# Graph-network megakernel on Trainium2: adjacency products of the first stage moved ahead, bias terms in two buffers on three engines

## What is computed

```python
def L0(x, adj_in, adj_out, bias_in, bias_out, gate_w_in, gate_b_in, gate_w_out, gate_b_out, loop_gate):
    msg_in  = (einsum('nm,bmd->bnd', adj_in, x)  + bias_in)  * sigmoid(x @ gate_w_in  + gate_b_in)
    msg_out = (einsum('nm,bmd->bnd', adj_out, x) + bias_out) * sigmoid(x @ gate_w_out + gate_b_out)
    msg_loop = x * sigmoid(x @ loop_gate)
    return relu(msg_in + msg_out + msg_loop)
def L1(features, A, W1, ...):
    A_norm = A + eye(n)
    deg = A_norm.sum(0) + A_norm.sum(1) - diagonal(A_norm)
    A_hat = A_norm * rsqrt(deg)[:, None] * rsqrt(deg)[None, :]
    agg = einsum('nm,bmd->bnd', A_hat, features)
    h = relu(batchnorm(agg @ W1.T + b1)); ...
x = layernorm(x + L0(x, adj, adj, ...))
x = layernorm(x + L1(x, adj, ...))
x = layernorm(x + L2(x, adj, ...))
x = layernorm(x + L3(x, adj, ...))
```

## Time and profile before

| | us |
|---|---|
| median of three runs | 679.86 |
| lowest and highest | 679.27, 680.56 |
| the profiled execution | 680.88 |
| its span, first to last instruction | 678.9 |
| mean granted TensorE clock | 0.989 |

### The profile page before, as it was taken

How to read it: one execution, slowest core, us unless ns; L and a number is a source line. 1 busy time by engine, 2 the same in 40 slices (tenths; PEclk the granted TensorE clock), 3 DMA queues, 4 the chain that set the end, 5 groups by cost and what they waited for, 6 DMA issues and landing times.

```text
span 678.9 us, 9236 instructions
## 1 busy us (share of the span) xinstructions
PE 632.6 (93%) x2698; PEld 435.5 (64%) x2698; DVE 475.9 (70%) x1510; ACT 426.8 (63%) x921; POOL 243.6 (36%) x262
## 2 busy tenths in 40 slices
PE   7899988997799999999999999999999999999993
PEld 5655746445585587578657757765775686576572
DVE  5977885778886657876876787688668765463354
ACT  3667766764846676675667577666857666446552
POOL 4599982004644031324506232440523243021031
PEclk7999999999999999999999999999999999999997
DMA  8224000000000000000000000000000000000000
GB/s 339 94 96 180 4 1 0 1 0 1 0 1 1 0 1 1 1 1 31 2 0 1 31 1 1 31 1 0 2 31 1 1 31 1 0 2 31 1 31 31
DMA packets 4225, 16.80 MB, mean 25 GB/s; under 512 B 464, under 2 KB 464, under 8 KB 4048
## 3 DMA queue, kind: packets, MB, share of 16 engines
q1 hardware_dynamic: 4176, 16.23, 6.2%
HBM read 12.03 MB, written 4.19 MB: 24 GB/s over the span
## 4 chain that ended last, share of the span: by engine, by line
PE 60%; DVE 13%; ACT 7%; issue 3%; POOL 1%; DVEq 0%; ACTq 0%; POOLq 0%
PE QQ L783 23%; PE QQ L795 14%; PE QQ L634 4%; PE PA L738 4%; PE PA L766 4%; PE PB L757 2%; DVE raw L1472 2%; ACT raw L1044 2%; DVE HT L1450 2%; ACT raw L1051 2%; DVE raw L1468 2%; ACT HB L1012 2%; PE PB L719 1%; PE PB L805 1%; PE PA L719 1%
## 5 line engine op out<-in xcount | busy, mean ns | idle before, releaser
L1044 ACT ACTIVATE raw<-QQ,BL 128x256 f32<-128x256 f32 (+2 forms) x312 | 168.8, 562 | 95.5 <-PE QQ L795 53.9
L783 PE MATMUL QQ<-HT,WT 128*128 128x256 f32 (+2 forms) x624 | 206.1, 473 | 7.7 <-DVE HT L1484 3.9
L783 PEld LDWEIGHTS QQ<-HT,WT 128*128 128x128 f32 x624 | 115.3, 190 | 75.4 <-issue 30.2
L384 POOL TENSOR_TENSOR RSD<-VAR,pw 128x8 f32<-128x8 f32 (+1 forms) x42 | 62.0, 1475 | 238.9 <-DVE VAR L1224 238.9
L795 PE MATMUL QQ<-HB,WT 128*128 128x256 f32 (+2 forms) x384 | 114.7, 442 | 3.0 <-DVE HB L1484 2.7
L1462 DVE SCALAR_TENSOR_TENSOR raw<-raw 128x512 f32<-128x512 f32 (+2 forms) x88 | 51.5, 585 | 64.7 <-ACT raw L1044 64.0
L795 PEld LDWEIGHTS QQ<-HB,WT 128*128 128x128 f32 x384 | 70.0, 190 | 37.7 <-issue 15.3
L498 POOL TENSOR_TENSOR HB<-HB 128x512 f32<-128x512 f32 x28 | 35.1, 1276 | 131.8 <-ACT HB L1002 131.8
L1051 ACT ACTIVATE raw<-raw 128x512 f32<-128x512 f32 (+2 forms) x88 | 45.1, 512 | 50.5 <-DVE raw L1472 39.9
L1484 DVE SCALAR_TENSOR_TENSOR HB<-raw 128x256 f32<-128x256 f32 (+2 forms) x48 | 24.0, 501 | 30.8 <-ACT raw L1051 30.8
L905 ACT ACTIVATE X<-Z,OFF,RSD 128x128 f32<-128x128 f32 x88 | 35.1, 481 | 8.8 <-POOL OFF L390 8.7
(11 more groups left out here) (208 smaller groups left out, 1090.5 us busy)
## 6 DMA issues: line engine op xcount, KB each, us to landing
raw<-in_xt SPq DMA_DIRECT2D x8, 512.0 KB, 6.6
four<-in_x SPq DMA_DIRECT2D x8, 512.0 KB, 5.3
out<-four SPq DMA_DIRECT2D x7, 512.0 KB, 2.6
WT<-in_lstm SPq DMA_DIRECT2D x1, 2048.0 KB, 9.4
later<-in_later SPq DMA_DIRECT2D x1, 725.5 KB, 10.0
AD<-in_adj SPq DMA_DIRECT2D x1, 512.0 KB, 6.3
out<-four SPq DMA_DIRECT2D x2, 256.0 KB, 2.1
early<-in_early SPq DMA_DIRECT2D x1, 274.0 KB, 2.9
```

Of the source, the lines that this page charges most:

```text
L384: pool.tensor_tensor(RSD[kk][:, ts], VAR[kk][:, ts], pw[:, ts], ALU.pow).then_inc(ln[k]["rstd"], some)
L783: mm = pe.matmul(steps_view(Q[q], k), WT[:, 0, (p - 1) * 4 + q, :], ht_view(par, k), start=True, stop=(s == 0))
L1044: act.activation(TG[q][:, 0:n], Q[q][:, 0:n], ACT.Tanh, scale=0.5 if q == G else 0.25, bias=BL[:, p - 1, q:q + 1]).then_inc(g_ok, 1)
```

## The change

TensorE makes the adjacency products of groups 0, 1 and 2 before the first spread; group 1's goes to the other PSUM buffer QA. From then on `neighbours(g + 1)` stands between the gate scores and `widen(g - 1)`, no longer behind it. The row sums and the score vectors go behind the last widening. Seven spins stand behind the first gate scores; those ahead of the first and of the last spread are gone, and of twelve behind the stage six are left.

The transposed half of the adjacency is loaded first, under a semaphore of its own, and the diagonal comes with the early constants, so that VectorE needs no reductions for it. U and V2 have two buffers each. GpSimd makes the first half of bias_in g0 and ScalarE the second (from group 2 on), GpSimd makes bias_out g1. Groups 0 to 2 have V2 added on VectorE. ScalarE evicts two widened pieces ahead of the apply and two behind it, then makes the loop term and its half of the bias. A spread signals after each half. On VectorE the statistics of a widened group come one group later, and the copies of the score vectors ahead of the output stage.

```diff
             sp.dma_start(early[:], early_in).then_inc(early_ok, 16)
             load_xt(0)
-            sp.dma_start(AD[:], adj).then_inc(adj_in, 16)
+            sp.dma_start(AD[:, 1], adj[:, 1]).then_inc(adjt_in, 16)
             load_x(0)
+            sp.dma_start(AD[:, 0], adj[:, 0]).then_inc(adj_in, 16)
             load_xt(1)
             load_x(1)
+            load_xt(2)
+            load_x(2)
             sp.dma_start(later[:], later_in).then_inc(later_ok, 16)
...
-            rstd(0, 0, 0)
-            two_terms(1)
-            sum_two(1)
-            biases(2)
-            rstd(0, 1, 1)
-            both_biases(2)
-            with_loop(2)
-            for g in range(2, GROUPS):
-                if g + 1 < GROUPS:
-                    biases(g + 1)
-                    both_biases(g + 1)
-                rstd(0, g % 2, g)
-                if g + 1 < GROUPS:
-                    with_loop(g + 1)
+            second(1)
+            rstd(0, 0, 0)
+            sum_two(1)
+            first_half(2)
+            second(2)
+            sum_two(2)
+            rstd(0, 1, 1)
+            for g in range(APART, GROUPS + 1):
+                if g < GROUPS:
+                    first_half(g)
+                    second(g)
+                    both_biases(g)
+                rstd(0, (g - 1) % 2, g - 1)
+                if g < GROUPS:
+                    with_loop(g)
...
             def spread(g):
...
-                if g == GROUPS - 1:
-                    pe.wait_ge(gate_z, GROUPS)
-                    spin(Q[3][:, 0:P], 8)
...
-                mm.then_inc(agg1_ps, 1)
+                    if b % 2:
+                        mm.then_inc(agg1_ps, 1)
...
             spin(Q[0][:, 0:P], 8)
             gates(0)
-            pe.wait_ge(adj_in, 16)
+            spin(Q[0][:, 0:P], 7)
+            pe.wait_ge(adjt_in, 16)
             neighbours(0)
             gates(1)
-            row_sums()
+            gates(2)
             neighbours(1)
             turn_adj()
-            vectors()
-            gates(2)
-            spin(Q[0][:, 0:P], 4)
+            neighbours(2)
             for g in range(1, GROUPS + 1):
-                if 1 < g < GROUPS:
-                    neighbours(g)
                 spread(g - 1)
                 if g + 2 < GROUPS:
                     gates(g + 2)
+                if 2 < g + 1 < GROUPS:
+                    neighbours(g + 1)
                 widen(g - 1)
...
             squash(2)
             norm_apply(0, 0, ZS[0], 0, X1[:, 0])
+            loops(2)
+            first_bias(2)
             for g in range(1, GROUPS + 1):
-                if g + 1 < GROUPS:
-                    loops(g + 1)
                 hidden(g - 1)
+                widened(g - 1, (0, 1))
                 if g + 2 < GROUPS:
                     squash(g + 2)
                 norm_apply(0, g % 2, ZS[g % 2], g, X1[:, g]) if g < GROUPS else None
+                widened(g - 1, (2, 3))
+                if g + 2 < GROUPS:
+                    loops(g + 2)
+                    first_bias(g + 2)
...
             dve.wait_ge(adj_in, 16)
-            dve.wait_ge(ident_ok, 1)
-            for c in range(NC):
-                s = slice(c * P, (c + 1) * P)
-                done(dve.tensor_tensor_reduce(DGS, ADJ[:, c, s], ident[:], 1.0, 0.0, ALU.mult, ALU.add, deg[:, 2, c:c + 1]))
             done(dve.tensor_reduce(deg[:, 0, :], ADJ, AX.X, ALU.add))
-            done(dve.tensor_reduce(deg[:, 1, :], ADJT, AX.X, ALU.add))
...
+                if g == 0:
+                    gate_out(1)
                 dve.scalar_tensor_tensor(out=z[:], in0=z[:], scalar=0.0, in1=XIN[:, g % NX], op0=ALU.max,
                                          op1=ALU.add).then_inc(mix3, 1)
-                if g == 0:
-                    gate_out(1)
```

More of the change, by code:

```diff
@@ L71 @@
 _at = 0
-for _name, _n in (("GW", 4), ("GBI", NC * GB * 4), ("BIO", 2 * NC * P)):
+for _name, _n in (("GW", 4), ("GBI", NC * GB * 4), ("DG", NC), ("BIO", 2 * NC * P)):
     EARLY[_name] = (_at, _n)
@@ L160, in build @@
         GBI = first("GBI")
+        DG = first("DG")
         BIO = first("BIO").rearrange("p (k c d) -> p k c d", k=2, c=NC)
@@ L318, in nth, with near, firsts @@
             return buf[:, t * P:(t + 1) * P]
+        def near(g):
+            return QA if g == 1 else PB
         def upto(n):
             return min(n, GROUPS)
+        APART = 3
+        def firsts(g):
+            return TILES * (g + 1) if g < 2 else 2 * TILES + GB * (g - 1)
         def slots(slot):
@@ new lines, in second, with sum_two @@
+            def second(g):
+                pool.wait_ge(gate_g, g + 1)
+                reach(pool, mix2, min(g - 1, APART))
+                reach(pool, bias_ok, g - 1 - APART)
+                pool.tensor_tensor(by_tile(V2[g % 2][:]), wide(1), gate(g, 1), ALU.mult).then_inc(second_ok, 1)
+            def sum_two(g):
+                pool.wait_ge(second_ok, g + 1)
+                pool.wait_ge(loop0_ok, 1) if g == 0 else pool.wait_ge(loop_ok, TILES * g)
+                pool.tensor_tensor(V2[g % 2][:], V2[g % 2][:], U[g % 2][:], ALU.add).then_inc(both_ok, 1)
@@ L435, in with_loop @@
-                pool.wait_ge(loop_ok, TILES * (g + 1))
-                pool.tensor_tensor(V[g % 2][:], V[g % 2][:], U[:], ALU.add).then_inc(both_ok, 1)
+                pool.wait_ge(bias_ok, g + 1 - APART)
+                pool.wait_ge(loop_ok, TILES * g)
+                pool.tensor_tensor(V[g % 2][:], V[g % 2][:], U[g % 2][:], ALU.add).then_inc(both_ok, 1)
             pool.wait_ge(early_ok, 16)
-            two_terms(0)
+            second(0)
+            pool.wait_ge(x_in[0], 16)
+            pool.tensor_tensor(by_tile(U[0][:]), by_tile(XIN[:, 0]), gate(0, 2), ALU.mult).then_inc(loop0_ok, 1)
@@ L440, in _ @@
             sum_two(0)
             pool.wait_ge(deg_ok, 2)
[L442 removed]
+            pool.tensor_tensor(dinv[:], deg[:, 2, :], pw[:, 0:NC], ALU.pow).then_inc(dinv_ok, 1)
             for c in range(NC):
@@ L553, in vectors @@
             def vectors():
-                pe.wait_ge(later_ok, 16)
-                pe.matmul(Q[2][:, 0:P + 1], WTR, AR[:, P - 1:2 * P], start=True, stop=True).then_inc(setup_pe, 1)
+                for k in range(2):
+                    pe.matmul(Q[3][:, k * P:(k + 1) * P], AR[:, k * P:(k + 1) * P], WTR, start=True, stop=True)
+                pe.matmul(PB[:, 0:P + 1], WTR, AR[:, P - 1:2 * P], start=True, stop=True).then_inc(setup_pe, 1)
             def gates(g):
@@ L617, in _ @@
                     gates(g + 2)
+                if 2 < g + 1 < GROUPS:
+                    neighbours(g + 1)
                 widen(g - 1)
             pe.wait_ge(gate_z, GROUPS)
-            for k in range(2):
-                mm = pe.matmul(Q[3][:, k * P:(k + 1) * P], AR[:, k * P:(k + 1) * P], WTR, start=True, stop=True)
-            spin(Q[3][:, 2 * P:3 * P], 12)
+            row_sums()
+            vectors()
+            spin(PA[:, 0:P], 6)
             pe.wait_ge(hid_ok, 4 * GROUPS)
@@ L941, in hidden, with widened @@
                     for q in range(2):
+                        act.wait_ge(agg1_ps, 2 * g + q + 1)
                         act.activation(AG[:, q * BANK:(q + 1) * BANK], PA[:, q * BANK:(q + 1) * BANK], ACT.Copy).then_inc(agg1_ok, 1)
-                for r, (q, h) in enumerate(pieces(g)):
+            def widened(g, some):
+                for r in some:
+                    q, h = pieces(g)[r]
                     n = 4 * g + r
@@ L1266, in _ @@
                 mix(g)
+                if g + 2 < GROUPS:
+                    gate_sum(g + 2)
                 if g == 0:
-                    setup_late()
-                elif g + 2 < GROUPS:
-                    gate_sum(g + 2)
+                    scaled_turned()
+                if g >= 2:
+                    hidden_stats(g - 2, range(4))
+                if g + 2 < GROUPS:
                     gate_out(g + 2)
-                if g >= 1:
-                    hidden_stats(g - 1, range(4))
             setup_last()
+            hidden_stats(GROUPS - 2, range(4))
             step = [0]
@@ L1611 @@
     gbi[:, :, :, 0:2] = spread[:, :, None, :]
-    early = [L0_gnn_gate_w_in, L0_gnn_gate_w_out, L0_gnn_loop_gate, none, gbi.reshape(P, -1),
+    early = [L0_gnn_gate_w_in, L0_gnn_gate_w_out, L0_gnn_loop_gate, none, gbi.reshape(P, -1), nodes(np.diagonal(adj))[:, :, 0],
              nodes(L0_gnn_bias_in).reshape(P, -1), nodes(L0_gnn_bias_out).reshape(P, -1)]
```

118 lines of the change are left out of this document (54 added, 64 removed).

## The result

The changed kernel takes 683.31 us (median of five runs, 681.81 to 685.05) where the kernel before takes 679.47 beside it (five runs, 679.03 to 680.56). The ratio is 1.0053, 95% interval 1.0035 to 1.0072: slower by 3.8 us. The forecast was 677.2, with a range that ended at 681.2. The profiled execution is the changed kernel's quickest, 681.81 us with a span of 680.0 and a mean granted clock of 0.990. Of the ten executions of the changed kernel in this study (five here, five in e12) only two had that clock; the other eight had 0.981 to 0.984 and took 682.51 to 685.05 us, so that e12's profile, further down, is of the commoner kind.

What follows compares the result with a forecast made beforehand. TensorE was taken to bound the first stage, GpSimd just behind. Spread 2 came 5.6 us earlier, slower cycles left 2.0 at the last spread, halves added 0.68: sum 2.7, so 677.2 us, range 673.8 to 681.2.

Steps and rivals of the forecast that it cites:

- What bounds the kernel: First stage: TensorE sets the pace with GpSimd just behind; TensorE's new loop is 12.3 us a group.
- The head: Start to spread 2: earlier input and filler keeping the clock up let spread 2 start 5.6 us earlier.
- last rival: Clock falls twice, among the early gate scores and at the last spread: 682.0 us, slower; chance 0.15.
- third rival: Head gives little: GpSimd's sum takes the lock before the last degree step, costing 2.5 us: 679.7; chance 0.11.
- The lock: VectorE on two SBUF operands and GpSimd exclude each other for whole instructions; whoever waits already goes first.
- The steady cycle: Groups 3 to 6: apply to apply through ScalarE and GpSimd takes 13.1 us against 12.1 to 12.4 before.
- The last spread: End of the first stage: starts at 111.7 us, 2.0 earlier, and takes 3.7 us at full clock.
- The likeliest case: The forecast itself, 677.2 us, with the last spread at full clock; chance 0.40.
- the rivals: Cases with a clock fall at the last spread, 2.85 us lost: alone 680.0 (chance 0.16), with a second fall 682.0 (0.15).
- The clock among the gate scores: Between the first two adjacency products: a clock fall there makes neighbours 1 2.6 us longer, apply(1) 2.0 later.
- Halves: Last spread signals by halves, so the widening starts 3.72 instead of 4.40 us behind it: 0.68 us gained.
- Score vectors' copies: Three copies (0.9 us) on VectorE ahead of the output stage: hidden if VectorE is not late, otherwise 0.9 once.

Runs made afterwards that it cites:

- e12: The changed kernel run and profiled again with nothing edited; 683.16 us, ratio to before 1.0041.
- e2: Changed kernel with ScalarE's half of the first bias ahead of its loop term from group 3 on; 678.19 us, ratio to before 0.9973.
- e5: Changed kernel with bias tiles ahead of loop tiles and 16 filler passes ahead of the last spread; 679.48 us, ratio to before 0.9992.
- e10: Changed kernel where, from group 3 on, GpSimd adds second bias and loop term behind the roots and VectorE adds that sum; 677.03 us.
- e8: Changed kernel with bias tiles first, filler among the gate scores and ahead of the last spread, none at the head; 674.69 us.
- e3: Changed kernel without the seven filler products behind the first gate scores; 683.14 us, ratio to before 1.0047.
- e4: Changed kernel with six filler products (12 passes) between the gate scores of groups 1 and 2; 680.01 us, ratio to before 0.9999.
- e1: Changed kernel with eight filler products (16 passes) put back ahead of the last spread; 684.92 us, ratio to before 1.0065.
- e7: Changed kernel with bias tiles first, 12 filler passes among the gate scores and 16 ahead of the last spread; 675.24 us.
- e11: As e8, but with group 2's adjacency product behind the first spread and group 3's gate scores; 677.89 us, ratio to before 0.9953.
- e9: As e8, but without the 16 filler passes ahead of the last spread; 674.82 us, ratio to before 0.9912.
- e6: Changed kernel with bias tiles first and 12 filler passes between the gate scores of groups 1 and 2; 674.85 us.

## Why the prediction was wrong, point by point

**What bounds the kernel.** Right: where nothing else interferes the stage runs at TensorE's own loop, forecast 12.3 us, 12.29 in e2 and in every later kernel with the bias tiles first.

**The head: the step that failed.** "Seven filler products (14 passes of about 0.11 us) cover 6.82 to 8.35, so the clock should stay up and the product take 3.6 us: it ends at 12.3 instead of 15.87", and behind it "neighbours 1 by 20.2". Both products were costed at full clock, and both ran at half clock for a part or all of their length. The term was -5.6 us at spread 2 and measured -0.9 (-1.6 in e12), which is 4.0 to 4.7 of the 5.5 us between forecast and measured sum.

The mistake was to put the fall in the earlier trace rows down to the idle time behind 6.82, which filler would cover. In both executions of the changed kernel TensorE was busy without a break from 1.03 us on, and in e12 the granted clock fell all the same, while the filler was running:

```profile
8.00:9.00 1.00, 1.00 (x5) 0.50 1.06 430
```

The same was recorded in e2, e5 and e10, the other three profiled with this filler and gate scores 0 of 1.95 us. What those executions share with the kernel before is the gate scores of group 0 ahead of the fall, as the prediction's own last rival had it; every kernel here has them, so that they are the cause is not shown. In the first profile gate scores 0 took 3.57 us and the filler 0.24 us a pass, and filler at that speed is itself a queue in front of the product. The first products of all executions profiled took 4.3 to 6.5 us; none took 3.6.

The two profiles lose the time at different places. In the first, the product ends 4.0 us late (16.3), group 0's mix starts 4.0 late, and the apply of group 1 comes 4.8 late. In e12 the product ends only 1.2 late (13.5) and the first apply is at 23.70, 0.5 late. There it is the second product, 5.38 us at half clock, that costs: the turned adjacency is done at 23.7 instead of 20.7, VectorE waits for it, and group 1's mix starts 3.5 late:

```profile
23.77 0.48 DVE L1205 TENSOR_SCALAR AHT<-PA,dinv 128x256 f32<-128x256 f32 x1 [2.08 <-PE PA L562]
...
26.17 2.16 DVE L1261 SCALAR_TENSOR_TENSOR X<-QQ,GS,one_a 128x128 f32<-128x128 f32 x8
```

The second spread starts 2.7 late and takes 1.4 longer, and spread 2 is again 4.0 late (52.80 instead of 48.8). With filler among the gate scores, none at the head and the bias tiles first (e8), spread 2 starts at 50.81, the earliest of all profiles and still 2.0 late.

The rest of the chain was sized well where the second product didn't stand in its way: mix of group 0 to its apply 10.8 forecast, 11.5 measured in the first profile (16.44 to 27.92, with a relu step that waited 1.7 us for the lock) and 10.1 in e12; apply 0 to apply 1 12.2 forecast and 12.3 in the first profile (27.92 to 40.19), but 14.4 in e12. The last degree step, forecast to be in at 11.65, ended at 11.66 in e12; in the first profile it waited for a GpSimd product and ended at 13.24, nearly as the third rival had it, but the late product hid that. VectorE's rows of the first profile for these, the degree step, the mix and the relu step of group 0:

```profile
11.41 1.83 DVE L1198 SCALAR_TENSOR_TENSOR deg<-deg,early 128x2 f32<-128x2 f32 x1
16.44 2.16 DVE L1261 SCALAR_TENSOR_TENSOR Z<-PB,GS,one_d 128x128 f32<-128x128 f32 x8 [3.20 <-PE PB L586]
...
20.30 2.95 DVE L1272 SCALAR_TENSOR_TENSOR Z<-Z,four 128x1024 f32<-128x1024 f32 x1
```

**The lock.** Right, as in the SUM of 2.22 us above. By the rule of the Trainium skill that the prediction named (SBUF — State Buffer, "SBUF: two separate sides"), the traces agree.

**The steady cycle.** Right: 13.1 forecast, 12.90 measured, in the pieces named (root 0.80 us behind the add; bias tiles 1.27, forecast 1.2). e2 and e10 show from two sides that GpSimd's add in front of the roots was the cause. From spread 2 to the last spread +3.6 was forecast. +2.9 came, since four cycles took 12.9 and not 13.1 us, and +2.2 in e12, where the first of them, behind the second spread at half clock, took 12.3.

**The last spread.** The likeliest case had it at full clock; it ran at half clock behind 3.2 us of idle time in every profiled execution of the changed kernel and of e3 and e4, and took 1.6 to 3.0 us more (the rivals said up to 2.85). The removed sixteen passes had held the clock, as e1, e5, e7, e8 and e11 show. In the traces this delays the output stage; in no pair of medians did the filler bring it back (see e9), so what it costs in time is not shown.

**The clock among the gate scores.** The last rival, at 0.15, named this fall and the one at the last spread together, and gave 682.0. Both happened, and the median came at 683.31. The second product took 5.1 to 6.7 us in all seven executions profiled without filler there, and 3.68 in all six with it.

**Halves.** Right: the widening starts 3.75 us behind the last spread in e7 (111.22 to 114.97), forecast 3.72, before 4.40. **Score vectors' copies.** Costed at nothing, and the output stage waits for ScalarE's eviction (1.68 us, L996), as it did.

**The odds.** The two clock falls had been priced as one case of 0.15, on top of a first product that ran at full clock. Both were there in each of the two profiles, and the first product was slow as well.

## What to carry to other kernels

Where TensorE does little but gate scores and waiting, as between the first two products here, and behind an idle stretch like the 3.2 us ahead of the last spread, cost the next dense product at half clock too; but cost filler itself at half speed at the start of a program, and don't take it for granted that it holds the clock there. When a product is pulled ahead, write down what it hides: the third product here was worth about 3 us because it filled a wait ahead of the first spread, while behind that spread it stood in the widening's way. When work is handed from one engine to a second, look at what the first had queued behind it: four bias tiles behind eight loop tiles cost 4 us in the traces and 5 in the medians, and swapping the two lines gave them back.

## What the runs showed of the hardware that was not expected

**The start has two phases.** Gate scores 0, the same sixteen passes at about 4.9 us, took 1.95 to 2.08 us in seven of fourteen profiled executions (before, e2, e5, e9 to e12) and 3.57 to 3.58 in the other seven; the changed kernel, profiled twice, shows both. The granted clock in the records is 1.00 from 8 to 12 us of the changed kernel's first profile, while filler took 0.24 us a pass there and 0.13 at 17.6 us in e4. So at a program's start a granted clock of 1.00 in the records doesn't mean full speed; lengths of instructions do. A busy DMA does not explain the slow passes: its share was 1.02 there, and 1.03 from 15 to 17 us in e9, where a pass took 0.13.

```profile
8.00:12.00 4.00, 4.00 (x18) 1.00 1.02 418
```

The Trainium skill (TensorE: Matmul & The Clock Gate, "What's actually happening") holds that the throttled state is the default until activity releases it and that the start varies from run to run; by that rule, the lengths agree, and the recorded clock does not.

**The same idle time, two outcomes.** Behind 2.66 us of idle time a last spread took 3.69 us (e9), behind 2.68 us 5.21 and 5.38 (e2, e6). Behind 1.86 or 1.87 us the second spread took 3.69 in six executions, behind 2.09 us it took 3.69 in e2 and 5.38 in e3. A chance belongs to such a stretch, not a yes or no.

**A tail that varies by itself.** From the start of the output stage to the end the same instructions took 550.9 to 552.7 us. An edit worth 1 us ahead of it, such as the last filler, can't be seen in five runs.
